# Four transformer layers on one core: the Mamba and expert stage with routers beside expert blocks, smaller exp blocks and a new order of pieces

## The chip, the cores and the metric

One Trainium2 chip, one of its cores. The metric is the device time of one execution in microseconds (us); lower is better.

## The reference, cut to what matters

`x` is 2 x 1024 tokens of 128 channels. Eight sub-layers follow each other, each as `x = x + layernorm(f(layernorm(x)))`. The change touches the first two:

```
# 1: Mamba, then a residual and a mixture of 8 experts, top 2
h  = rmsnorm(x);  xm, z = split(h @ W_in.T)          # 256 channels each
xc = silu(causal_conv4(xm) + conv_b)
dt, B, C = split(xc @ W_xproj.T)                     # 64, 16, 16
delta = softplus(dt @ W_dt.T + b_dt)                 # 256 channels
h[n] = exp(delta * A[n]) * h[n] + delta * B[n] * xc  # 16 states n, scanned along the tokens
y  = sum over n of h[n] * C[n] + D_skip * xc
x1 = x + (y * silu(z)) @ W_out.T
out = x1 + sum over 8 experts of w[e] * (silu(g @ gate[e]) * (g @ up[e])) @ down[e],  g = rmsnorm(x1)
# 2: 64 small experts (hidden 32, top 8) and 2 shared ones (hidden 256)
out = sum over e of c[e] * (silu(g @ W1[e] + B1[e]) @ W2[e] + B2[e]) + shared(g)
```

The others are an RWKV layer with a ternary projection, attention in a window of 32 with position-routed linear maps, and attention in Lorentz space with an MLP of one shared and 8 routed experts.

## The kernel before, in words

The 2,048 tokens are four groups of 512, held in SBUF as `X`. Every engine walks through one and the same list of pieces, `ORDER` (lines 95 to 149), and issues its own part of each piece; nothing else sets the order. A piece is a lane, a step and a group: `aF1.0` is step F1 of lane a for group 0. Queues run in order, so a wait in one piece holds up all pieces behind it on that engine. Waits are on semaphores that count steps, with group numbers folded in (`at_least`).

Lane a (`mamba_and_experts`) is the subject. Its **Mamba steps** for group i: F1, F5, F6 normalise (statistics and scaling on VectorE, the power on GpSimd, transposes on TensorE; L608 to L630); F2 and F0 project in, L441 and L444; F7 convolves, L642 and L644, and applies Silu; F3 projects to dt, B and C; F8 projects to delta, L456, and takes the softplus on ScalarE (Abs, Exp, Ln, L357 to L367) and VectorE; F4 spreads the first B row over the partitions (L461) with a selector matrix `sel`; F9 makes `delta * xc`. Then there are 16 states k: `Nk` makes the C row in PSUM bank S0 (L468), which ScalarE copies to `cb` (L371), and VectorE multiplies delta x with the B row in bank S2 (L691); `Aq` makes eight of the 32 exps of `delta * A` on ScalarE (L377); `nk` has two scans on VectorE (L698) into one of the buffers `hs` and the next B row (L471); `ok` keeps the last column for the next group with a VectorE copy (L703, groups 0 and 2, since a batch is two groups), multiplies `hs` with `cb` on GpSimd (L313) and adds the product to `cv` (L290). B1, B3, B4 and B2 gate, project out, add the residual and normalise. The normalised `XA` is kept for the experts.

Its **expert steps** for group e: R1, R3, R4 route to 8 experts (logits in bank E0, softmax and top 2 on VectorE, transposes in E0, three bf16 parts of the weights in `w3`); M0 to M15 are the blocks of the 8 experts, two for each: spread weight in bank E3 (L504), gate L507, up L510, Silu L399, product L752, down L557, and the weighing L854; L1 and L3 to L5 sum up and normalise; R2, R5, R6 route to 64 experts; U0 to U15 are four small experts each (L537, L543 and L544, Silu L414, product L809, down L563), U16 to U19 the shared ones; L2, L6, L7 end the layer. The Mamba of group g stands beside the experts of group g-1 in the list; the experts of group 3 stand beside the first RWKV pieces (lane b, steps K), the rest of which stand among the window attention (steps A, Q, C, N, V, H, W, O, X). Lane c is the last layer.

ScalarE holds one set of function tables at a time, and an ACT_TABLE_LOAD is issued where the next function is of another set (Exp, Ln, Silu). The selectors `sel` (96 x 4096) and `selE` (128 x 2048) are built by GpSimd in F5 of group 0, by four memsets and five selects (L259 to L270); semaphore `selectors` counts them. Two lines which the prediction follows:

```
L377  act.activation(dA[...], dl[...], ACT.Exp, scale=Aneg[...])       # for t in range(8 * k, 8 * k + 8)
L703  inc(V.tensor_tensor(carry[:, k, :], hs[:, k % HS, :, G - 1], hs[:, k % HS, :, G - 1], ALU.max))
```

Of the kernel before, what the change touches and what calls it, by code (L numbers as in the profile page):

```python
# [89 lines left out]
MAMBA_END = 130016  # L90
# [2057 lines left out]
```

## Time and profile before

| | us |
|---|---|
| median of 3 runs (1591.90 to 1593.06) | 1592.79 |
| the profiled execution | 1592.28 |
| its span in the trace | 1590.5 |
| TensorE busy | 1170.1 (74%) |
| VectorE busy | 1098.0 (69%) |
| ScalarE busy | 636.9 (40%) |
| GpSimd busy | 540.1 (34%) |

The profile is one execution. The trace lists each instruction with its engine (PE is TensorE, PEld its weight loads, DVE VectorE, ACT ScalarE, POOL GpSimd), the line of the kernel, the tiles, the start and the duration; an idle engine's row names what ended the idle time. PEclk is the granted TensorE clock as a share of full speed. The groups' Mamba fronts (F1) begin near 5, 150, 327 and 503 us; lane a's Mamba ends near 668 us, group 3's experts near 835 us.

### The profile page before, as it was taken

Reading aid. Unit: us, or ns where it says so; the run is one execution under the profiler, and the core shown is the slowest. Engines: PE = TensorE matmul, PEld = TensorE weight load, DVE = VectorE, ACT = ScalarE, POOL = GpSimd, SP = SyncE. Lnnn points to the kernel's source line nnn. Section 1 sums busy time; section 2 is a strip of 40 time slices with the busy share of each in tenths; the row PEclk is TensorE's granted clock in tenths of the full one; section 3 lists DMA queues with packets and bytes.
Section 4 is the critical chain, followed back from the end, with each engine's and each line's share of the span. In section 5 each row is a group of like instructions: output and inputs, shape, how many; then the busy total and the mean of one; then the engine's idle time right before and its main releaser. Section 6 shows DMA issues by size and latency. Waiting matters only on the chain.

```text
span 1590.5 us, 12969 instructions
## 1 busy us (share of the span) xinstructions
PE 1170.1 (74%) x3808; PEld 564.8 (36%) x3818; DVE 1098.0 (69%) x2497; ACT 636.9 (40%) x1147; POOL 540.1 (34%) x348
## 2 busy tenths in 40 slices
PE   2223784967477774969597686787978699999897
PEld 1001232323223331334233352435435255555553
DVE  6896787669897788666827898997787644444221
ACT  2530763337332663332321421413325056654443
POOL 6495185515753185601202222131321012112111
PEclk8555896978789896969797898998999899999999
DMA  5000000000000000020001000000000100000000
GB/s 190 0 0 0 0 1 0 1 0 1 0 1 0 1 1 0 7 85 0 1 0 60 1 1 1 1 1 1 0 1 1 60 0 1 7 1 7 1 7 7
DMA packets 11270, 17.75 MB, mean 11 GB/s; under 512 B 1304, under 2 KB 7584, under 8 KB 10688
## 3 DMA queue, kind: packets, MB, share of 16 engines
q1 hardware_dynamic: 11200, 16.93, 3.1%
q8 instruction: 30, 0.49, 0.1%
q14 instruction: 40, 0.33, 0.1%
HBM read 15.88 MB, written 1.05 MB: 11 GB/s over the span
## 4 chain that ended last, share of the span: by engine, by line
PE 30%; DVE 17%; ACT 3%; issue 2%; POOL 1%; POOLq 0%; DVEq 0%; ACTq 0%
PE bankE L1682 7%; PE bankE L1760 5%; DVE b_yt L1477 2%; PE bankE L1148 2%; PE bankS L1709 2%; PE bankS L1724 1%; DVE b_m L1436 1%; PE bankE L537 1%; DVE b_pT L1449 1%; PE bankE L1169 1%; PE bankS L1662 1%; DVE b_vh L1285 1%; PE bankE L563 1%; DVE c_tw L1852 1%; DVE b_xnS L1256 1%
## 5 line engine op out<-in xcount | busy, mean ns | idle before, releaser
L313 POOL TENSOR_TENSOR hc<-hs,cb 128x1024 f32<-128x1024 f32 x60 | 141.1, 2352 | 77.9 <-DVE hs L698 75.2
L698 DVE TENSOR_TENSOR_SCAN hs<-dA,carry,bankS 128x512 f32<-128x512 f32 x128 | 156.5, 1263 | 3.0 <-ACT dA L377 0.9
L1682 PE MATMUL bankE<-c_h,c_w 128*128 128x512 f32 x288 | 151.3, 608 | 7.7 <-DVE c_tw L1852 6.1
L1655 ACT ACTIVATE c_h<-bankE,C 128x512 f32<-128x512 f32 x144 | 99.0, 688 | 118.2 <-PE bankE L1760 117.9
L290 POOL TENSOR_TENSOR cv<-cv,hc 128x1024 f32<-128x1024 f32 x60 | 141.5, 2358 | 4.7
L1852 DVE SCALAR_TENSOR_TENSOR c_tw<-bankE,C,wb_ready 128x512 f32<-128x512 f32 x32 | 24.0, 750 | 123.3 <-PE bankE L1682 123.3
L1551 POOL TENSOR_TENSOR c_acc<-c_acc,c_tw 128x512 f32<-128x512 f32 x32 | 40.7, 1273 | 185.3 <-DVE c_tw L1852 185.3
L414 ACT ACTIVATE sg<-bankE,C 128x512 f32<-128x512 f32 x80 | 55.0, 687 | 120.8 <-PE bankE L537 120.8
L1760 PE MATMUL bankE<-c_fH,c_w1H 128*128 128x512 f32 x144 | 101.1, 702 | 0.0
L537 PE MATMUL bankE<-fT,f 128*128 128x512 f32 x128 | 76.1, 678 | 13.6 <-DVE c L802 13.6
L471 PE MATMUL bankS<-bc,sel 96*128 96x512 bf16 x60 | 28.9, 481 | 72.1 <-DVE hs L698 72.1
L377 ACT ACTIVATE dA<-dl,Aneg 128x512 f32<-128x512 f32 x128 | 80.1, 708 | 0.1
L691 DVE TENSOR_TENSOR bankS<-dx,bankS 128x1024 f32<-128x1024 f32 x64 | 78.1, 1220 | 1.0 <-PE bankS L471 0.8
L507 PE MATMUL bankE<-h2T,wg 128*128 128x512 f32 x128 | 72.3, 648 | 7.5 <-ACT sg L399 7.5
L1062 ACT ACTIVATE b_pr<-bankE,b_nm 128x160 f32<-128x160 f32 x128 | 48.4, 404 | 72.5 <-DVE b_nm L1438 72.5
L371 ACT ACTIVATE cb<-bankS 128x512 f32<-128x512 f32 x64 | 37.9, 592 | 93.4 <-PE bankS L468 93.4
L563 PE MATMUL bankE<-hh,f 128*128 128x512 f32 x128 | 69.6, 626 | 5.1 <-DVE hh L809 5.1
L557 PE MATMUL bankE<-hh,wd 128*128 128x512 f32 x128 | 67.7, 611 | 2.5 <-DVE tw L854 2.0
L1682 PEld LDWEIGHTS bankE<-c_h,c_w 128*128 128x128 f32 x288 | 51.4, 190 | 33.4 <-issue 15.4
L313 POOL TENSOR_TENSOR cv<-hs,cb 128x1024 f32<-128x1024 f32 x4 | 9.4, 2357 | 147.8 <-DVE hs L698 147.8
L1760 PE MATMUL bankE<-c_fL,c_w1H 128*128 128x512 f32 x144 | 57.7, 401 | 0.0
L1760 PE MATMUL bankE<-c_fH,c_w1L 128*128 128x512 f32 x144 | 57.5, 399 | 0.0
(483 smaller groups left out, 2738.9 us busy)
## 6 DMA issues: line engine op xcount, KB each, us to landing
c_w<-in_w SPq DMA_DIRECT2D x1, 2304.0 KB, 8.9
X<-in_x SPq DMA_DIRECT2D x4, 256.0 KB, 3.7
wg<-in_gate_T SPq DMA_DIRECT2D x1, 1024.0 KB, 7.7
wu<-in_up_T SPq DMA_DIRECT2D x1, 1024.0 KB, 9.9
f<-in_w SPq DMA_DIRECT2D x1, 1024.0 KB, 7.2
out<-X SPq DMA_DIRECT2D x4, 256.0 KB, 2.3
b_wq<-in_Wqkv SPq DMA_DIRECT2D x1, 768.0 KB, 4.4
g<-in_sw SPq DMA_DIRECT2D x2, 256.0 KB, 3.4
```

Of the source, the lines that this page charges most:

```text
L290: pool.tensor_tensor(cv[:, :, :], cv[:, :, :], hc[:, :, :], ALU.add).then_inc(s["y_acc"], 1)
L313: pool.tensor_tensor(dst[:, :, :], hs[:, k % HS, :, :], cb[:, k % 2, :].unsqueeze(1).to_broadcast([P, HV, G]), ALU.mult).then_inc(s["hc_re ...
L377: act.activation(dA[:, t % DA, :], dl[:, h, :], ACT.Exp, scale=Aneg[:, h * NS + n:h * NS + n + 1]).then_inc(s["dA_ready"], 1)
L507: pe.matmul(E[0][:, :], wg[:, k * P:(k + 1) * P], h2T[:, :], start=True, stop=True).then_inc(s["g_ready"], 1)
L537: pe.matmul(E[k % 2][:, :], w, fT[:, :], start=True, stop=True).then_inc(s["up_ready"], 1)
L557: mm = pe.matmul(E[2][:, :], wd[:, b, :], hh[:, b % 2, :], start=(b % FB0 == 0), stop=(b % FB0 == FB0 - 1))
L563: pe.matmul(E[2][:, :], f2[:, b, :], hh[:, b % 2, :], start=(b == 0), stop=False).then_inc(s["fdown"], 1)
L691: V.tensor_tensor(dbx[:, :, :], dx[:, :, :], S[2][:, :].unsqueeze(1).to_broadcast([P, HV, G]), ALU.mult).then_inc(s["dbx_done"], 1)
L698: V.tensor_tensor_scan(hs[:, k % HS, h, :], dA[:, (HV * k + q) % DA, :], dbx[:, h, :], carry[:, k, h:h + 1], ALU.mult, ALU.add).then_inc(s ...
L1655: act.activation(h[:, n % 3, :], E[k % 2][:, :], ACT.Gelu_apprx_tanh, bias=col("b1_3", k)).then_inc(s["c_h"], 1)
L1682: pe.matmul(E[2][:, :], w2[:, k, :], h[:, n % 3, :], start=(f == 0), stop=(f == FB3 - 1)).then_inc(s["c_down"], 1)
L1760: mm = pe.matmul(E[k % 2][:, :], wp[:, k * P:(k + 1) * P], fp[:, i % 2, :], start=(q == 0), stop=(q == 2))
```

## The change

- **Selectors.** GpSimd adds parts of the identity into `cb`, and ScalarE spreads them into `sel` and `selE` with two copies before its first piece.
- **Group 0.** For states 3, 7, 11 and 15 VectorE multiplies `hs` by the C row in PSUM into a new buffer `hv`; ScalarE's copy to `cb` and GpSimd's product fall away there.
- **Carry.** The copy of the last column is a ScalarE copy.
- **First normalisation.** Statistics, powers and result have their own buffers (`stF`, `mvF`, `powF`, `rsF`, `tF`, `xnF`); VectorE's part of F6 is in F5; `XA` holds two groups, so F5 of group i waits for step L4 of group i-2. `oT` is `hT`.
- **F8, F4, F9.** The delta projection writes banks S0 and S2 and doesn't wait for the split of B and C; the first B row is made in F9, after delta.
- **Routers.** They use bank E3, not E0; the gates of the M blocks and the spread weights share E0 and E3 in a ring; a weight is spread one expert later, so M0 and M1 need no router result. The shared experts are U0 to U3. `sg` has three buffers. The weighing moves behind the odd block.
- **Exps.** Four instead of eight in a piece: A0 to A7.
- **ORDER** is laid out anew (999 pieces for 983), in all lanes. In groups 1 to 3, R3 and R4 stand further back (in groups 2 and 3 between F8 and F4), two M blocks stand between F4 and F9. `F1` of a group stands right behind `B2` of the group before, as it did. RWKV pieces K4.1 to K17.1 stand among U5.3 to U17.3.

The start of the list before and after, and the code:

```diff
-    aF1.0 aF5.0 aF6.0 aF2.0 aF0.0 aF7.0 aF3.0 aF8.0 aF4.0 aF9.0 aN0.0 aA0.0 an0.0 ao0.0 aN1.0 an1.0 ao1.0 aN2.0 an2.0 ao2.0 aN3.0 aA1.0
-    aB3.0 aB4.0 aB2.0 aF1.1 aR1.0 aF5.1 aR3.0 aF6.1 aF2.1 aF0.1 aR4.0 aF7.1 aM0.0 aF3.1 aM1.0 aM2.0 aF8.1 aF4.1 aF9.1 aM3.0 aN0.1 aM4.0
-    aA0.1 an0.1 ao0.1 aN1.1 an1.1 aM5.0 ao1.1 aN2.1 aM6.0 an2.1 aM7.0 ao2.1 aN3.1 aM8.0 aA1.1 an3.1 ao3.1 aN4.1 an4.1 aM9.0 ao4.1 aN5.1
...
+    aF1.0 aF5.0 aF6.0 aF2.0 aF0.0 aF7.0 aF3.0 aF8.0 aF4.0 aF9.0 aA0.0 aN0.0 an0.0 ao0.0 aN1.0 an1.0 ao1.0 aA1.0 aN2.0 an2.0 aA2.0 ao2.0
+    an15.0 ao15.0 aB1.0 aB3.0 aB4.0 aB2.0 aF1.1 aR1.0 aF5.1 aM0.0 aF6.1 aF2.1 aF0.1 aR3.0 aF7.1 aR4.0 aM1.0 aF3.1 aF8.1 aF4.1 aM2.0 aM3.0
+    aF9.1 aA0.1 aN0.1 an0.1 aM4.0 ao0.1 aM5.0 aN1.1 an1.1 aM6.0 aM7.0 ao1.1 aA1.1 aN2.1 an2.1 aM8.0 ao2.1 aN3.1 aM9.0 an3.1 aA2.1 aM10.0
...
+    def by_vector(i, k):
+        return i == 0 and k % 4 == 3
...
-            for q in range(3):
-                pool.wait_ge(s["selectors"], n)
-                pool.affine_select(out=sel[:, :, :], in_=sel[:, :, :], compare_op=ALU.not_equal, fill=1.0, base=-32 * q,
-                                   pattern=[[-1, 32], [0, P]], channel_multiplier=1).then_inc(s["selectors"], 1)
...
+        for ins in (pool.tensor_tensor(cb[:, 0, 0:32], ident[:, 0:32], ident[:, 32:64], ALU.add),
+                    pool.tensor_tensor(cb[:, 0, 64:128], ident[:, 0:64], ident[:, 64:128], ALU.add),
+                    pool.memset(w3[:, :], 0.0), pool.memset(p16[:, :, :], -1.0)):
+            ins.then_inc(s["selectors"], 1)
...
+        act.wait_ge(s["selectors"], 5)
+        act.activation(sel[:, :, :], cb[0:96, 0, 0:32].unsqueeze(2).to_broadcast([96, 32, P]), ACT.Copy).then_inc(s["selectors"], 1)
...
+            elif p[0] == "o" and not ends_batch(i):
+                at_least(act, s["scan_done"], i, HV * NS, HV * (k + 1))
+                act.activation(carry[:, k, :], hs[:, k % HS, :, G - 1], ACT.Copy).then_inc(s["carry_kept"], 1)
             elif p[0] == "A":
-                for t in range(8 * k, 8 * k + 8):
+                for t in range(EXPS * k, EXPS * k + EXPS):
...
             elif p == "F8":
                 at_least(pe, s["dt_ready"], i, 1, 1)
-                at_least(pe, s["bc_split"], i, 1, 1)
-                for h in range(HV):
-                    pe.matmul(S[h][:, :], wdt[:, h * P:(h + 1) * P], dtT[:, :], start=True, stop=True).then_inc(s["dpre_ready"], 1)
-            elif p == "F4":
-                if i == 0:
-                    pe.wait_ge(s["selectors"], 9)
+                for h in range(HV):
+                    pe.matmul(S[2 * h][:, :], wdt[:, h * P:(h + 1) * P], dtT[:, :], start=True, stop=True).then_inc(s["dpre_ready"], 1)
+            elif p == "F9":
+                if i == 0:
+                    pe.wait_ge(s["selectors"], 7)
                 at_least(pe, s["bc_split"], i, 1, 1)
+                at_least(pe, s["delta_ready"], i, HV, HV)
                 pe.matmul(S[2][:, :], sel[:, 0, :], bc3[:, :], start=True, stop=True).then_inc(s["Bb_ready"], 1)
...
-            elif p[0] == "o":
+            elif p[0] == "o" and by_vector(i, k):
                 at_least(V, s["scan_done"], i, HV * NS, HV * (k + 1))
-                if not ends_batch(i):
-                    inc(V.tensor_tensor(carry[:, k, :], hs[:, k % HS, :, G - 1], hs[:, k % HS, :, G - 1], ALU.max))
+                at_least(V, s["Cb_ready"], i, NS, k + 1)
+                at_least(V, s["y_acc"], i, NS - 1, k - 4)
+                V.tensor_tensor(hv[:, :, :], hs[:, k % HS, :, :], S[0][:, :].unsqueeze(1).to_broadcast([P, HV, G]), ALU.mult).then_inc(s["hv_ready"], 1)
```

## Rows read from the trace of the kernel before

**Rows 1.** Busy time by stretch: start:end, length; then PE, PEld, DVE, ACT, POOL, clock.

```profile
57.00:137.00 80.00, 15.52 (x30) 1.97 (x30) 73.12 (x64) 27.08 (x46) 72.66 (x31) 0.50 0.00 0
150.00:191.00 41.00, 29.24 (x66) 12.80 (x65) 28.08 (x70) 21.55 (x31) 2.04 (x2) 0.77 0.00 1
191.00:327.00 136.00, 99.22 (x251) 38.56 (x253) 105.22 (x177) 59.62 (x92) 85.71 (x42) 0.86 0.00 0
368.00:503.00 135.00, 97.78 (x238) 37.98 (x241) 120.50 (x172) 58.20 (x90) 84.64 (x41) 0.85 0.00 0
503.00:549.00 46.00, 31.52 (x78) 13.87 (x77) 32.42 (x90) 24.45 (x35) 3.02 (x3) 0.81 0.00 1
549.00:668.00 119.00, 86.63 (x217) 33.79 (x220) 96.50 (x138) 54.70 (x85) 83.61 (x40) 0.84 0.00 0
668.00:835.00 167.00, 131.99 (x337) 57.42 (x339) 99.24 (x292) 52.18 (x79) 23.48 (x25) 0.83 0.06 22
835.00:1120.00 285.00, 212.22 (x981) 115.84 (x982) 241.35 (x664) 82.05 (x268) 67.10 (x61) 0.89 0.03 9
1290.00:1590.50 300.50, 278.46 (x936) 157.57 (x934) 100.85 (x296) 159.33 (x232) 53.68 (x45) 0.99 0.01 4
```

**Rows 2.** The timeline, group 0's start and group 1's convolution: start, duration, instruction.

```profile
4.21 0.23 ACT L329 ACTIVATE Aneg<-C 128x32 f32<-128x32 f32 x1 [2.19 <-DMA C<-in_cst]
...
7.31 1.11 DVE L623 TENSOR_SCALAR XA<-X,mvS,rsS 128x128 f32<-128x128 f32 x4
...
8.55 5.92 DVE L628 TENSOR_SCALAR xnS<-XA,rsS 128x128 f32<-128x128 f32 x4
...
14.71 11.78 POOL L265 TENSOR_SCALAR_AFFINE_SELECT sel<-sel 96x4096 bf16<-96x4096 bf16 x3
...
19.37 7.40 DVE L642 TENSOR_SCALAR cv<-xm,C 128x512 f32<-128x512 f32 x2 [4.90 <-ACT xm L345]
...
26.63 5.18 POOL L270 TENSOR_SCALAR_AFFINE_SELECT selE<-selE 128x2048 bf16<-128x2048 bf16 x2
26.69 8.30 DVE L644 SCALAR_TENSOR_TENSOR cv<-xm,C,cv 128x512 f32<-128x512 f32 x6
...
162.62 0.49 DVE L642 TENSOR_SCALAR cv<-xm,C 128x512 f32<-128x512 f32 x1 [1.54 <-ACT xm L345]
...
164.72 4.06 DVE L644 SCALAR_TENSOR_TENSOR cv<-xm,C,cv 128x512 f32<-128x512 f32 x6
```

**Rows 3.** Instruction groups: busy, mean ns; then L703's, ns least/median/most.

```profile
L698 DVE TENSOR_TENSOR_SCAN hs<-dA,carry,bankS 128x512 f32<-128x512 f32 x128 | 156.5, 1263 | 3.0 <-ACT dA L377 0.9
...
L691 DVE TENSOR_TENSOR bankS<-dx,bankS 128x1024 f32<-128x1024 f32 x64 | 78.1, 1220 | 1.0 <-PE bankS L471 0.8
...
L371 ACT ACTIVATE cb<-bankS 128x512 f32<-128x512 f32 x64 | 37.9, 592 | 93.4 <-PE bankS L468 93.4
...
L703 DVE TENSOR_TENSOR carry<-hs x32: 155/1216/2315, 59.1 to 487.0; 128x2 f32<-128x2 f32 x32
```

**Rows 4.** The timeline of group 1's front.

```profile
170.99 0.59 ACT L357 ACTIVATE dtT<-bankS 64x512 f32<-64x512 f32 x1 [0.47 <-PE bankS L450]
...
176.25 1.98 PE L456 MATMUL bankS<-dtT,wdt 64*128 64x512 f32 x4
...
189.44 1.28 ACT L377 ACT_TABLE_LOAD   x1
190.73 5.01 ACT L377 ACTIVATE dA<-dl,Aneg 128x512 f32<-128x512 f32 x8
```

**Rows 5.** Waits, 150 to 327 us: in total, times, longest.

```profile
DVE hh L752 <- ACT sg L399: 5.4, 8, 1.6
...
PE bankE L495 <- DVE wt L834: 4.1, 1, 4.1
PE bankE L529 <- DVE wt L791: 4.0, 1, 4.0
```

**Rows 6.** A wait of 690 to 835 us, and VectorE's busy time in 852 to 905.

```profile
DVE hh L809 <- PE bankE L544: 15.9, 8, 3.2
...
852.00:905.00 53.00, 38.98 (x120) 0.76 0.12 45
```

More of the change, by code:

```diff
@@ L195, in mamba_and_experts, with rows_by @@
     cb = sb("cb", [P, 2, G])
+    hv = sb("hv", [P, HV, G])
+    def by_vector(i, k):
+        return i == 0 and k % 4 == 3
+    def rows_by(vector, i, k):
+        return sum(by_vector(i_, k_) == vector for i_ in range(i + 1) for k_ in range(NS if i_ < i else k))
     carry = sb("carry", [P, NS, HV])
-    oT = sb("oT", [P, G])
-    XA = sb2("XA", [P, NG * T * P])
+    oT = hT
+    XA = sb2("XA", [P, 2 * T * P])
     stE, mvE = sb2("stE", [P, T, 6]), sb2("mvE", [P, T, 2])
@@ L228, in mamba_and_experts @@
     N_M, N_U = E0N * FB0, EB1 + SB1
+    RING, BEFORE, held = {}, {}, {}
+    for n, tenant in enumerate([("gate", 0), ("gate", 1)] + [t_ for x_ in range(E0N) for t_ in (("weight", x_), ("gate", 2 * x_ + 2), ("gate", 2 * x_ + 3))][:-2]):
+        place = 0 if n < 2 or n % 2 else 3
+        RING[tenant], BEFORE[tenant] = E[place], held.get(place)
+        held[place] = tenant
     def sync(sp):
@@ L434, in piece @@
                 at_least(pe, s["xh_ready"], i, 1, 1)
-                turn(S[0], xnS).then_inc(s["xhT_ready"], 1)
+                turn(S[0], xnF).then_inc(s["xhT_ready"], 1)
             elif p == "F2":
@@ L522, in piece @@
                 at_least(pe, s["fT_ready"], e, 1, 1)
+                at_least(pe, s["wb_ready"], e, E0N, E0N)
                 for j in range(T):
-                    mm = pe.matmul(E[0][:, j * E1N:(j + 1) * E1N], fT[:, j * P:(j + 1) * P], r1[:, :], start=True, stop=True)
+                    mm = pe.matmul(E[3][:, j * E1N:(j + 1) * E1N], fT[:, j * P:(j + 1) * P], r1[:, :], start=True, stop=True)
                 mm.then_inc(s["lg_ready"], 1)
@@ L550, in piece, with ring_free, spread_weight @@
                 turn(E[0], yT).then_inc(s["moT_ready"], 1)
+        def ring_free(e, kind, n):
+            if BEFORE[kind, n] is not None:
+                was, m = BEFORE[kind, n]
+                at_least(pe, *((s["sg_ready"], e, N_M) if was == "gate" else (s["wb_ready"], e, E0N)), m + 1)
+        def spread_weight(e, x_):
+            if x_ == 0:
+                at_least(pe, s["w3_ready"], e, 2, 1)
+            ring_free(e, "weight", x_)
+            pe.matmul(RING["weight", x_][:, :], sel[:, x_, :], w3[:, :], start=True, stop=True).then_inc(s["wbc_ready"], 1)
         def down0(e, b):
@@ L668, in piece @@
                     at_least(V, s["sp_abs"], i, HV, h + 1)
-                    inc(V.tensor_scalar(dl[:, h, :], S[h][:, :], col("b_dt", h), 0.0, ALU.add, ALU.max))
+                    inc(V.tensor_scalar(dl[:, h, :], S[2 * h][:, :], col("b_dt", h), 0.0, ALU.add, ALU.max))
                 for h in range(HV):
@@ L758, in piece @@
                 at_least(V, s["moT_ready"], e, 2, 1)
-                inc2(V.tensor_tensor(xnE[:, :], XA[:, cols(e, 0, G)], E[0][:, :], ALU.add))
+                inc2(V.tensor_tensor(xnE[:, :], XA[:, cols(e % 2, 0, G)], E[0][:, :], ALU.add))
                 wait2()
```

309 lines of the change are left out of this document (158 added, 151 removed).

## The prediction

> **What bounds the kernel now.** I read the stretches first. Beside group 0's scans VectorE is busy 73.1 of 80 us and GpSimd 72.7, TensorE next to nothing. In the three cycles in which the Mamba of group g stands beside the experts of group g-1 (150 to 668 us) no engine is full: a front (F1 to F9) has 41 us with VectorE busy 28 and TensorE 29, the scans behind it 136 us with 105 and 99; group 2's scans hold 120 of VectorE in 135. Group 3's experts alone (668 to 835) lean on TensorE, 132 of 167, the window-attention stretch (835 to 1120) on VectorE, 241 of 285 or 85%, and the last 300 us are TensorE's, 278, so nothing in the change can shorten those but what comes earlier [rows 1]. Then the start: GpSimd builds the selectors until 31.8 us, and every VectorE row beside it is long [rows 2]. Then the repeated instructions by their groups [rows 3], the front of group 1 [rows 4], and the waits inside the first cycle [rows 5].
>
> **Part 1, selectors.** Three selects of 3.9 us each and more are replaced by small adds on GpSimd and two ScalarE copies. Beside GpSimd, xnS takes 5.92 us for four instructions, where XA, the same shape just before, takes 1.11: -4.8. The convolution runs from 19.37 to 34.99 us, where group 1's runs from 162.62 to 168.78: 15.6 less 6.2, -9.4 [rows 2]. The copies: 592 ns for 512 elements [rows 3] and 230 for 32 [rows 2] give 0.75 ns per element, so 3.3 us (4096) and 1.8 (2048). ScalarE is free near 4.9 us, so it is done near 10.0; hT would be wanted at 8.55 + 1.1 + 1.1 = 10.8. I take nothing; if the copies start late or run long, up to +5.1. First comes what the rows show: the long instructions are tensor_scalar and scalar_tensor_tensor while GpSimd works, and the same are short later. The Trainium skill (SBUF — State Buffer, section Who interferes with whom) says that such instructions in their two-port mode, or with two SBUF inputs, and GpSimd exclude each other for a whole instruction. By that rule the whole excess goes with the selects, as in my sum.
>
> **Part 2, F8.** The delta projection starts at 176.25 us although dtT stood at 171.6 [rows 4]; the B and C split and expert matmuls were between. In group 0 only the split was: -2.5, and -0.9 more for A0 placed before N0. The matmul that moves from F4 to F9 now waits for delta, which it did in effect before (its successor N0 did); behind it on TensorE stand N0 and the M blocks. Group 0's front: -4.8 -9.4 -2.5 -0.9 = **-17.6**.
>
> **Part 3, group 0's scans.** VectorE has per state one product 1.22, two scans 2.52 and a carry copy of 1.22 median; together 4.96, the pace of the stretch (80 / 16 = 5.0). GpSimd has 31 instructions, 72.66 us, so 2.34 each [rows 1, 3]. The change takes the copy to ScalarE (27 us busy of 80) and four products of GpSimd to VectorE, at the 1.22 us of the product with one PSUM operand. VectorE: 16 x 3.74 + 4 x 1.22 = 64.7; GpSimd: 27 x 2.34 = 63.2, plus 2.5 until the first scan ends. Each state hands over between the two, so I add about 5: 70.5, **-9.5** (bounds -6 if handovers cost double, -13 at 67). In those four states TensorE's next C row waits for VectorE's product, not for ScalarE's copy, and GpSimd's add behind it too; both are off the pace by a state and sit in the 5. The next scan of a buffer now waits for ScalarE's carry copy as well; it is short (32 elements took 0.23 us [rows 2]) and nothing but exps is queued behind it. With part 1 and 2: **-27** (-20 to -31).
>
> **Part 4, the paired cycles.** The first two expert blocks and the four shared blocks need no router result, so they cover what TensorE now spends waiting for the routers' weights, 4.1 + 4.0 us a cycle [rows 5]. F8 gives 2.5, the third sg buffer half of the 5.4 us that VectorE waits for Silu [rows 5], 2.7. Together 13.3: I take all in the first cycle, half in each of the next two, since group 2's scans are at 89% of VectorE and cannot take up more. The carry copies of group 2 (16 x 1.22 = 19.5 us) leave VectorE; a quarter of that, -5, since ScalarE's copy waits for the scans with Silus queued behind it. Against it F9, which waits behind M2 and M3: a Silu and a table load [rows 4], +2 in all. Sum -13 -7 -7 -5 +2 = **-30**.
> The exps: four blocks of eight (5.01 us and two loads of 1.28, so 7.57) become eight of four (2.5 + 2.56 = 5.07): ScalarE has 10.3 us more per cycle. By the order list 36 table changes up to B2 of group 3 become 50, and with the rest of the experts 15 more; 15 x 1.28 = 19 us of ScalarE. It is busy 81 of 177 in a cycle [rows 1], so it has room, and shorter blocks hold the Silus up less each time. The Trainium skill (ScalarE: Activation LUTs, sections What ACT_TABLE_LOAD costs and Rules for kernel authors) tells one to group by table set, and puts a switch at 2.66 us with its drain; it speaks against this part, and by it ScalarE would have 40 us more.
> Bounds of the cycles: 0, if each freed wait only uncovers the next; -56, if VectorE fills them to the 85% of the attention stretch: its busy time is 133 (150 to 327) + 149 (a front's 28 and group 2's 120.5) + 129 (503 to 668), less 19.5 for the carries, 391 / 0.847 = 462 against 518 [rows 1].
>
> **Part 5, the rest of the order.** Group 3's experts gain the two router waits (-8), but K-lane pieces (K4.1 to K17.1) come in among the U blocks: TensorE +4; **-3** (-8 to +2). Those pieces leave the attention stretch; in the part that holds them VectorE has 39 us of work in 53 [rows 6], about a third theirs, 13: **-10** (-4 to -16). Some of layer 3 starts earlier: **-4** (0 to -8), as the end is TensorE's. The new buffers, XA of two groups (F5 waits for L4 of group i-2, which is long done) and F6's VectorE part inside F5: nothing, VectorE does the same work in the same place. No DMA is added or moved, so SP's queue is as it was; on GpSimd the pow instructions keep their places among the pieces, now free of the selects ahead of them.
>
> Sum: -27 -30 -3 -10 -4 = -74, from the profiled execution's 1592.3 us (span 1590.5), 0.5 under the median 1592.8: **1518 us**.
>
> **The rivals.**
> 1. **The cycles don't shorten.** VectorE in F9 waits for the Silus of M2 and M3 which now stand ahead, or hh waits for TensorE, as in group 3's experts, 15.9 us over eight [rows 6]; the routers' cover is used up by that. For it: no engine is full, so the chain passes between engines. Against: the waits in rows 5 are TensorE's. Sum without part 4: -44, 1548.
> 2. **The cycles shrink to VectorE.** Part 4 at -56: -100, 1492. For it: the whole order is laid out anew, not only the named waits. Against: GpSimd, busy 86 of 136 us in the scans with instructions of 2.34 us, must hand over as well.
> 3. **Slower: ScalarE becomes the chain.** In the three cycles 24 breaks of 5.07 us stand where 12 of 7.57 did, 122 against 91, +31, and each F9 waits a Silu, a load and a hand back, about 4.5, +13. If TensorE and VectorE stand through every break and the rest gains nothing, -27 + 44: 1609. It decides from 27 us of ScalarE on the path. Against: ScalarE has 96 us free per cycle.
> 4. **It doesn't do what it says.** The first normalisation is to stand among the scans, but in the new list F1 of g+1 still comes right behind B2 of g, so no gain of it is in my sum. Were it among them, each of its tensor_scalars would stand beside GpSimd's products, and four cost 5.92 and not 1.11 us [rows 2]. That changes no number here.
>
> **How the numbers follow.** Forecast 0.50 (1500 to 1540, from the terms' bounds), rival 1 0.25, rival 2 0.20, rival 3 0.04, and 0.01 for all gains given back, within 0.2%, which is about what a measurement can tell from no change. Range: from rival 2, 1492 less 10 for its other terms' bounds, to rival 1, 1548 plus 14: 1482 to 1562. Faster 0.95, same 0.01, slower 0.04.
>
> **What would show it.** The first VectorE scan near 39 us, not 57; xnS near 1.1 us for four and the convolution near 6; group 0's last scan near 110; carry copies on ScalarE; the cycles, F1 to F1, at about 165, 165 and 159 us where they are 177, 176 and 165 (150, 327, 503, 668); no wait of TensorE for wt (L495 and L529 of before) over 1 us; ScalarE near 660 us busy; the last 300 us unchanged. Wrong: ScalarE's copies ending after 12 us; F9's matmul waiting over 5 us for delta; cycles as long as before (rival 1) or under 155 (rival 2); table loads between long idle times of TensorE (rival 3).

## The result and the profile after

The changed kernel takes 1546.31 us (median of 4 runs, 1544.80 to 1549.05); the kernel before took 1592.92 us beside it. The ratio is 0.9703 (95% interval 0.9677 to 0.9729), 46.6 us less. The span of the profiled execution fell from 1590.5 to 1543.6 us.

To see where the 46.9 us of span went I cut both traces at one VectorE instruction that occurs once in a group: the sum of XA and the projected Mamba output in B4, "XA<-XA,bankS". It starts at 144.7, 320.8, 498.3 and 668.3 us before, and at 113.3, 280.6, 451.4 and 624.7 after (first and last start stand in these two rows, before and after):

```profile
L717 DVE TENSOR_TENSOR XA<-XA,bankS x4: 686/686/687, 144.7 to 668.3; 128x512 f32<-128x512 f32 x4
L756 DVE TENSOR_TENSOR XA<-XA,bankS x4: 680/684/689, 113.3 to 624.7; 128x512 f32<-128x512 f32 x4
```

So group 0 gave 31.3 us, the cycles of groups 1 to 3 gave 8.9, 6.6 and -3.3 (176.1, 177.5 and 170.0 before; 167.2, 170.9 and 173.3 after), and everything behind gave 3.3 (922.2, 918.9). Of the 12.2 us of the cycles, 10.4 lie in the fronts, from the cut to the next group's first scan (46.8, 47.5 and 50.9 us before; 41.8, 45.0 and 48.0 after).

Busy time by stretch of the kernel after, columns as in [rows 1]:

```profile
35.00:113.00 78.00, 20.06 (x37) 3.83 (x38) 65.40 (x56) 27.48 (x59) 63.39 (x27) 0.51 0.00 0
118.50:155.00 36.50, 26.97 (x62) 11.28 (x61) 26.89 (x71) 21.26 (x30) 2.04 (x2) 0.78 0.00 1
155.00:286.00 131.00, 98.32 (x251) 38.25 (x252) 105.13 (x165) 66.77 (x99) 85.08 (x41) 0.90 0.00 1
325.50:457.00 131.50, 99.73 (x248) 39.52 (x249) 104.81 (x162) 69.28 (x116) 85.02 (x41) 0.88 0.00 0
499.00:625.00 126.00, 96.83 (x245) 37.96 (x247) 100.73 (x141) 67.18 (x99) 83.97 (x40) 0.91 0.00 0
625.00:791.00 166.00, 125.78 (x331) 55.72 (x333) 110.80 (x329) 53.09 (x81) 25.35 (x27) 0.86 0.06 22
791.00:1073.00 282.00, 218.41 (x987) 121.68 (x986) 232.47 (x637) 82.43 (x270) 66.39 (x63) 0.87 0.03 9
1243.00:1543.60 300.60, 277.91 (x936) 158.78 (x934) 104.47 (x311) 158.19 (x231) 54.30 (x46) 0.97 0.01 4
```

Against [rows 1]: in group 0's scans VectorE is busy 65.4 and GpSimd 63.4 us, where they were 73 each. Group 2's scans have lost 16 us of VectorE's work (104.8 for 120.5), but only 3.5 us of their length (131.5 for 135). The last 300 us are as they were.

The start, timeline of the kernel after, to compare with [rows 2]:

```profile
4.99 3.62 ACT L347 ACTIVATE sel<-cb 96x4096 bf16<-96x4096 f32 x1
...
8.51 1.89 ACT L348 ACTIVATE selE<-cb 128x2048 bf16<-128x2048 f32 x1
8.62 0.87 DVE L663 TENSOR_SCALAR xnF<-XA,rsF 128x128 f32<-128x128 f32 x4
...
14.31 0.49 DVE L677 TENSOR_SCALAR cv<-xm,C 128x512 f32<-128x512 f32 x1 [4.81 <-ACT xm L359]
...
16.42 4.06 DVE L679 SCALAR_TENSOR_TENSOR cv<-xm,C,cv 128x512 f32<-128x512 f32 x6
```

ScalarE's two copies end at 10.40 us, 0.36 us before it is needed. xnF takes 0.87 us for four and the convolution is over at 20.48, not 34.99. Waits of TensorE in the three cycles of the kernel after (118 to 625 us):

```profile
PE bankE L449 <- DVE xnE L631: 36.8, 3, 12.7
PE bankE L593 <- DVE tw L894: 25.7, 21, 2.0
...
PE bankE L516 <- DVE wt L874: 4.5, 2, 2.2
```

and of the kernel before (150 to 668 us), the routers' two:

```profile
PE bankE L529 <- DVE wt L791: 13.7, 3, 5.6
...
PE bankE L495 <- DVE wt L834: 11.0, 3, 4.1
```

The routers' 24.7 us have become 4.5; in their place TensorE stands 25.7 us, 21 times, before the down projection (L593) for the weighed tile `tw`. That looks like the place where the gain of the cycles went. The run e_weigh says that it isn't.

### The profile page after: what moved, and what is told of

Same layout as the page of the kernel before. It is cut to its first block, busy times and chain, and to the rows that moved or that the text cites. A ratio compares the mean times of both kernels' runs of the same rounds, so it can differ in the third digit from the quotient of the medians.

```text
span 1543.6 us, 13061 instructions
## 1 busy us (share of the span) xinstructions
PE 1172.5 (76%) x3806; PEld 570.5 (37%) x3818; DVE 1059.8 (69%) x2469; ACT 660.3 (43%) x1191; POOL 508.6 (33%) x340
## 4 chain that ended last, share of the span: by engine, by line
PE 31%; DVE 15%; ACT 3%; issue 2%; POOL 0%; POOLq 0%; DVEq 0%; ACTq 0%
PE bankE L1722 8%; PE bankE L1800 5%; PE bankE L1188 3%; DVE b_yt L1517 2%; PE bankS L1764 2%; DVE b_m L1476 1%; PE bankS L1749 1%; PE bankE L1209 1%; DVE b_pT L1489 1%; PE bankE L599 1%; PE bankS L1239 1%; ACT b_pr L1102 1%; DVE c_tw L1892 1%; DVE b_pT L1296 1%; DVE b_vh L1325 1%
## 5 line engine op out<-in xcount | busy, mean ns | idle before, releaser
L324 POOL TENSOR_TENSOR hc<-hs,cb 128x1024 f32<-128x1024 f32 x56 | 131.7, 2352 | 59.0 <-DVE hs L735 56.5
L301 POOL TENSOR_TENSOR cv<-cv,hc 128x1024 f32<-128x1024 f32 x56 | 133.1, 2377 | 4.4
L593 PE MATMUL bankE<-hh,wd 128*128 128x512 f32 x128 | 70.2, 631 | 33.6 <-DVE tw L894 33.6
L525 PE MATMUL bankE<-h2T,wg 128*128 128x512 f32 x128 | 75.4, 674 | 6.3 <-ACT wb L438 6.3
L559 PE MATMUL bankE<-fT,f 128*128 128x512 f32 x128 | 72.1, 645 | 0.0
L1010 POOL TENSOR_TENSOR b_rsS<-b_powS,half 128x4 f32<-128x4 f32 x16 | 16.2, 1014 | 148.2 <-DVE b_powS L1284 148.2
L1722 PEld LDWEIGHTS bankE<-c_h,c_w 128*128 128x128 f32 x288 | 51.8, 190 | 32.8 <-issue 13.1
L385 ACT ACTIVATE cb<-bankS 128x512 f32<-128x512 f32 x60 | 35.2, 587 | 40.3 <-PE bankS L489 39.6
```

Of the source, the lines that this page charges most:

```text
L301: pool.tensor_tensor(cv[:, :, :], cv[:, :, :], (hv if by_vector(i, k) else hc)[:, :, :], ALU.add).then_inc(s["y_acc"], 1)
L324: pool.tensor_tensor(dst[:, :, :], hs[:, k % HS, :, :], cb[:, k % 2, :].unsqueeze(1).to_broadcast([P, HV, G]), ALU.mult).then_inc(s["hc_re ...
L525: pe.matmul(RING["gate", k][:, :], wg[:, k * P:(k + 1) * P], h2T[:, :], start=True, stop=True).then_inc(s["g_ready"], 1)
L559: pe.matmul(E[k % 2][:, :], w, fT[:, :], start=True, stop=True).then_inc(s["up_ready"], 1)
L593: mm = pe.matmul(E[2][:, :], wd[:, b, :], hh[:, b % 2, :], start=(b % FB0 == 0), stop=(b % FB0 == FB0 - 1))
L1722: pe.matmul(E[2][:, :], w2[:, k, :], h[:, n % 3, :], start=(f == 0), stop=(f == FB3 - 1)).then_inc(s["c_down"], 1)
```

## The experiments

Each row is one kernel, an edit of the changed one. The cuts are those of above; "rest" is from group 3's cut to the end of the span, us.

| run | median us | ratio to before (95%) | first scan | group 0's cut | cycles 1, 2, 3 | rest |
|---|---|---|---|---|---|---|
| before | 1592.9 | 1 | 56.7 | 144.7 | 176.1, 177.5, 170.0 | 922.2 |
| after | 1546.3 | 0.9703 (0.9677, 0.9729) | 35.6 | 113.3 | 167.2, 170.9, 173.3 | 918.9 |
| e_selectors | 1570.5 | 0.9859 (0.9825, 0.9893) | 51.1 | 129.4 | 169.3, 170.9, 173.3 | 922.3 |
| e_no_hv | 1562.1 | 0.9772 (0.9754, 0.9789) | 36.9 | 124.2 | 167.2, 172.6, 173.2 | 922.8 |
| e_carry | 1580.3 | 0.9875 (0.9822, 0.9929) | 35.3 | 121.4 | 168.3, 183.4, 176.4 | 930.7 |
| e_weigh | 1550.3 | 0.9739 (0.9705, 0.9772) | 36.5 | 114.4 | 166.5, 170.6, 173.3 | 933.6 |
| e_exps8 | 1573.4 | 0.9874 (0.9854, 0.9894) | 35.2 | 114.3 | 175.0, 173.5, 177.5 | 926.5 |
| e_router_back | 1581.4 | 0.9898 (0.9867, 0.9929) | 36.8 | 114.4 | 173.5, 178.0, 185.5 | 927.2 |
| e_m_after | 1575.1 | 0.9835 (0.9793, 0.9876) | 39.0 | 116.6 | 170.3, 174.4, 179.9 | 933.0 |
| e_norm_among | 1583.3 | 0.9911 (0.9880, 0.9943) | 38.6 | 123.3 | 177.6, 179.7, 176.4 | 930.5 |
| e_norm_gap | 1556.9 | 0.9744 (0.9725, 0.9763) | 37.5 | 116.8 | 173.8, 173.7, 173.9 | 920.7 |
| e_code_only | 1641.2 | 1.0291 (1.0268, 1.0314) | 38.7 | 117.1 | 200.9, 191.3, 194.5 | 937.4 |
| e_code_weigh | 1588.2 | 0.9942 (0.9919, 0.9964) | 38.7 | 117.1 | 187.0, 177.4, 179.2 | 932.6 |
| e_old_tail | 1556.8 | 0.9741 (0.9715, 0.9766) | 36.7 | 114.5 | 167.4, 172.7, 171.7 | 925.5 |

The kernel before, run beside the experiments, took 1594.1, 1599.6 and 1598.8 us in their three sets, so a ratio says more than a median; the expectations count from 1546. How far a number of the table repeats can be read from it: e_old_tail has the list of after up to R2 of group 3, and its cycles are within 2 us of it. The rest, however, is 919 us in after and 921 to 934 in the nine runs that leave the list behind that cut alone or nearly so. TensorE's clock explains most of that. These are the busy times of the rest in after and in e_weigh, columns as in [rows 1]:

```profile
624.70:1543.60 918.90, 759.73 (x2814) 410.66 (x2816) 572.99 (x1647) 346.64 (x710) 177.83 (x167) 0.91 0.03 11
624.80:1558.50 933.70, 774.94 (x2814) 418.25 (x2816) 574.96 (x1647) 346.74 (x710) 178.02 (x167) 0.89 0.03 11
```

The same 2,814 matmuls took 15.2 us longer at a granted clock of 0.89 than at 0.91, and the rest is nearly 15 us longer; e_m_after, e_carry and e_norm_among, the other three of the nine over 930, have a busy TensorE of 772.0, 769.6 and 768.9 us. (In e_router_back it is 758.2, so its 8 us are not the clock.) Such differences go into the ratios and medians, so I judge by the cuts. It also tells why medians lie above the times expected where the cuts agree with the forecast (e_selectors 1570.5 for at most 1568, e_no_hv 1562.1 for 1555): the expectations count from after, whose trace has one of the earliest starts and the shortest rest.

The start has a scatter of the same kind: nine of these runs leave the pieces up to the first scan as in after, and have it at 35.2 to 39.0 us. The last section shows why. Of the cut of group 0 and of the first scan only larger differences count, or such whose steps the trace shows.

### Group 0: selectors, products, carry

**e_selectors** puts GpSimd's four memsets and five selects back:

```diff
+                if i == 0:
+                    selectors()
...
-        act.activation(sel[:, :, :], cb[0:96, 0, 0:32].unsqueeze(2).to_broadcast([96, 32, P]), ACT.Copy).then_inc(s["selectors"], 1)
```

> The changed kernel with GpSimd's four memsets and five selects back in F5 of group 0 in place of the small adds and ScalarE's two copies. Forecast by my sum: xnF near 5.9 us for four, the convolution near 15 us long, the first scan 14 to 20 us later than the 35.6 us of the change; group 0's remaining work moves with it, since nothing later has slack to take it up: 1546 + 17 = 1563 (range 1558 to 1568). Rival: the delay is half absorbed, because the first group's scans then run beside a GpSimd that is not behind, or later groups catch up: 1550 to 1556.

Timeline of VectorE in this run:

```profile
8.09 5.92 DVE L671 TENSOR_SCALAR xnF<-XA,rsF 128x128 f32<-128x128 f32 x4
18.92 7.39 DVE L685 TENSOR_SCALAR cv<-xm,C 128x512 f32<-128x512 f32 x2 [4.90 <-ACT xm L367]
26.23 8.30 DVE L687 SCALAR_TENSOR_TENSOR cv<-xm,C,cv 128x512 f32<-128x512 f32 x6
```

The long rows of [rows 2] are back within 0.01 us, and the first scan is at 51.1, 15.5 us later than after; group 0's cut moves by 16.1, the first cycle is 2.1 us longer and the other two are the same. The forecast of the sum holds, the rival (half absorbed) falls. 1.4 of the 15.5 us are not VectorE's: from the start of F3's matmuls to `dtT` it is 3.38 us here and 1.97 in after, by the clock that the last section shows.

**e_no_hv** (`by_vector` returns False) and **e_carry** (below):

```diff
-            elif p[0] == "o" and not ends_batch(i):
-                act.activation(carry[:, k, :], hs[:, k % HS, :, G - 1], ACT.Copy).then_inc(s["carry_kept"], 1)
...
+                if not ends_batch(i):
+                    V.tensor_tensor(carry[:, k, :], hs[:, k % HS, :, G - 1], hs[:, k % HS, :, G - 1], ALU.max).then_inc(s["carry_kept"], 1)
```

> The changed kernel with all sixteen products of group 0 by C on GpSimd again. My sum: GpSimd's 31 instructions of 2.34 us take 72.6 us and set the pace at 4.7 us a state, where it is 4.0 now; group 0's first XA sum comes 8 to 10 us later than 113.3, and the cycles stay: 1546 + 9 = 1555. Rival (the scans and not GpSimd set the pace, as hs has several buffers): under 3 us.

> The changed kernel with the carry copy back on VectorE (two SBUF operands), in groups 0 and 2. My sum: group 0's scans go from 63 to about 76 us (16 copies of up to 1.22 us less what its slack hides, +10 to +16), group 2's cycle +5; 1546 + 18 = 1564. Rival: with the copy spread between the scans GpSimd, not VectorE, sets the pace in group 2, so that only group 0 grows: 1556 to 1560.

GpSimd at group 0's end in e_no_hv, timeline:

```profile
107.49 2.34 POOL L324 TENSOR_TENSOR hc<-hs,cb 128x1024 f32<-128x1024 f32 x1 [0.17 <-POOL cv L301]
109.91 2.34 POOL L301 TENSOR_TENSOR cv<-cv,hc 128x1024 f32<-128x1024 f32 x1
```

The busy times of its group 0, columns as in [rows 1]:

```profile
37.00:124.00 87.00, 21.28 (x38) 4.38 (x38) 60.20 (x51) 28.70 (x61) 72.68 (x31) 0.51 0.00 0
```

GpSimd's instructions stand back to back, 4.92 us a state; its last add is at 114.8 us, 12 us behind the last scan. From first scan to cut it is 87.3 us, where after has 77.7: the four products are worth 9.6, within the 8 to 10 expected, and the rival falls. The carry copies, in e_carry on VectorE and in after on ScalarE (ns least/median/most):

```profile
L737 DVE TENSOR_TENSOR carry<-hs x32: 147/950/2302, 37.8 to 463.6; 128x2 f32<-128x2 f32 x32
L388 ACT ACTIVATE carry<-hs x32: 189/204/206, 38.1 to 440.0; 128x2 f32<-128x2 f32 x32
```

In e_carry the distance from first scan to cut is 86.1, 8.4 more than after. In group 2's cycle the copies cost 12.5 us, where I had expected 5; the rival, by which only group 0 grows, falls. The two don't add up: before, with neither, the distance was 88.0, 10.3 more than after. A reason that fits the busy times of [rows 1] is that without either edit VectorE (73 us busy) and GpSimd (73) are equally late.

### The cycles: the weighing, the exp blocks, the router

**e_weigh**:

```diff
-                if k % FB0 == 1 and k > FB0:
-                    weigh(e, k // FB0 - 1)
                 if k >= 2:
                     at_least(V, s["down"], e, N_M, k - 1)
                 V.tensor_tensor(hh[:, k % 2, :], sg[:, k % SG, :], EU[k % 2][:, :], ALU.mult).then_inc(s["hh_ready"], 1)
+                if k % FB0 == 0 and k > 0:
+                    weigh(e, k // FB0 - 1)
```

> The changed kernel, but VectorE weighs expert x behind the product of block 2x+2, as before, and not ahead of the product of block 2x+3. In the trace after, TensorE waits for the weighed tile 7 times in each cycle, 8.3, 8.8 and 8.5 us, and 8.0 beside group 3; before, these waits were under 3 us. Theory A (the order puts the weighing behind a wait for the odd block's up projection, right ahead of the down projection that needs it, so TensorE stands once per expert and gives back what the routers saved): these waits fall to about 2 us a stretch, the cycles to about 161, 165 and 162 us, and the time to about 1546 - 22 = 1524. Theory B (the cycles go by the chain of scans and hand-overs on VectorE and GpSimd, TensorE has slack): the waits fall as well, the cycles stay within 2 us, 1543 to 1547. Theory C (VectorE is held up by a weighing that comes too early, since it waits for ScalarE's copy of the weight): waits of VectorE for wb of a us each, 1550 or more.

Waits of TensorE in its cycles, 118 to 625 us:

```profile
PE bankE L593 <- DVE tw L894: 12.7, 14, 1.3
```

The edit takes back the weighing of the changed kernel, which stands in the odd block ahead of its product, not behind the block as the description of the change says. The wait fell by 13.0 us, and group 3's cut stands at 624.8 against 624.7. Theory A falls, and so does my reading of the waits: 13 us of TensorE's waiting for `tw` were not on the path of any cycle. They were not won either: over the three cycles TensorE is idle for 126.7 us (510.4 less 383.7 busy), where it was 130.9 in after, so most of the idle time only came to stand before other instructions. Theory B holds for the cycles. The median of 1550.3 is above its 1543 to 1547; the profiled execution, at 1560.3, is the longest of the four, with the rest at the lower clock.

**e_exps8**: the same list, eight exps in every even piece, none in the odd. It also moves four of each eight exps forward to the piece before.

```diff
-                for t in range(EXPS * k, EXPS * k + EXPS):
+                for t in range(EXPS * k, EXPS * k + 2 * EXPS) if k % 2 == 0 else ():
```

> The changed kernel, but every even exp piece makes eight exps and every odd one none, so that the order is the same and the table changes fall by up to a half in the cycles. Theory A (the shorter blocks were worth having: Silu and copies wait 5.1 us and not 7.6 behind them): the cycles grow by 2 to 4 us each, 1550 to 1558. Theory B (the extra table loads take away as much as they give, the stated rule of grouping by table set holds): cycles shorter by 2 to 5 us each, 1532 to 1542, ScalarE's busy time down by about 15 us. Theory C (ScalarE has room either way): within 2 us, 1544 to 1548.

Table loads ahead of exps, first in e_exps8, then in the kernel after:

```profile
L394 ACT ACT_TABLE_LOAD  x13: 1283/1283/1283, 30.8 to 564.2; - x13
```

```profile
L394 ACT ACT_TABLE_LOAD  x19: 1283/1283/1283, 31.2 to 548.7; - x19
```

VectorE's wait for the Silus of the M blocks in the three cycles, in the same order:

```profile
DVE hh L793 <- ACT sg L412: 32.1, 15, 4.5
```

```profile
DVE hh L793 <- ACT sg L412: 15.3, 15, 4.2
```

ScalarE has 247.3 us of work in its three cycles and 263.0 in those of the kernel after, so fewer table changes do save it 16 us; and the cycles are 14.5 us longer. The wait of VectorE that grew most is the one for a Silu, by 16.8 us. Theory A has the sign right; the cycles grew by 7.8, 2.6 and 4.1 us, where it had 2 to 4. The edit doesn't part the length of the blocks from the place of the exps, and TensorE is busy 8.0 us longer on the same 933 matmuls (388.6 for 380.5), so how much of the 14.5 is the block length alone is open. The Trainium skill (ScalarE: Activation LUTs, section Rules for kernel authors) tells one to group by table set; the trace agrees that this saves ScalarE's time, and the cycles show that it didn't save the kernel's. The Trainium skill (ScalarE: Activation LUTs, section What ACT_TABLE_LOAD costs) puts a switch at 2.66 us, a load of 1.28 with a drain behind it. The drain is not seen in the trace after: at 26.04 us a load of 1.28 begins, and the next Exp starts at 27.34.

**e_router_back** moves R1, R3 and R4 of each group ahead of M0, which is also ahead of the next group's F6.

> The changed kernel with R1, R3 and R4 all ahead of M0 in each group. It measures the cover that M0 and M1 give the first router. Forecast of my sum: the 4.1 us wait of TensorE for wt comes back, and with it that of the parts of the weights, so +4 to +7 in each of three cycles, nothing beside group 3 (there the list has the router ahead of M0 anyway): 1558 to 1567. Rival (TensorE has slack in the cycles, as the weighing run showed: its waits fell by 13 us and no cycle moved): within 3 us, 1543 to 1549.

Waits of TensorE in it, 118 to 650 us:

```profile
PE bankE L517 <- DVE wt L875: 19.1, 3, 8.2
```

Cycles 6.3, 7.1 and 12.2 us longer, where I had expected 4 to 7; the rival (within 3 us in all) falls. Nearly all of it lies in the fronts, which take 46.7, 55.4 and 57.9 us for 41.8, 45.0 and 48.0. So the place of the router does count, unlike that of the weighing. The wait for `wt` grew by 14.6 us only (19.1 for 4.5), and the cycles by 25.7: the edit moves VectorE's and ScalarE's work of the router too, so the 25.7 us are the price of the whole move and not of that wait. What sets this wait apart, as the list has it, is what comes next behind it: the transposes and projections of the next group's front, which its scans need. That reason is argued, not shown by a run of its own.

**e_m_after** moves the M blocks between F4 and F9 behind N0.

> The changed kernel with the two M blocks that stand between F4 and F9 in groups 1 to 3 moved behind N0. My rival 1 blamed them: VectorE reaches delta times x of F9 only behind the products of both blocks, which wait for their Silus, and ScalarE's first exps come behind them. If so: from F8 to the first scan 4 to 6 us shorter, scans as long, 1546 - 12 = 1534. If they only fill the softplus chain, in which TensorE and VectorE would idle: the first scan is earlier, but the M blocks are later by as much, and the cycles grow by 0 to 5 us: 1546 to 1560.

VectorE in group 1's front:

```profile
150.76 1.23 DVE L728 TENSOR_TENSOR bankS<-dx,bankS 128x1024 f32<-128x1024 f32 x1
...
155.02 0.69 DVE L794 TENSOR_TENSOR hh<-sg,bankE 128x512 f32<-128x512 f32 x1 [3.03 <-ACT sg L413]
...
157.93 0.69 DVE L895 TENSOR_TENSOR tw<-bankE,wb 128x512 f32<-128x512 f32 x1 [2.22 <-PE bankS L529]
158.53 0.68 DVE L794 TENSOR_TENSOR hh<-sg,bankS 128x512 f32<-128x512 f32 x1
159.13 2.45 DVE L736 TENSOR_TENSOR_SCAN hs<-dA,carry,bankS 128x512 f32<-128x512 f32 x2
```

The product for the scan is made 11.7 us after `dtT` (139.1) and 18.1 in the kernel after (135.7, 153.8), so F9 did wait 6 us for the two blocks. But the scan then waits for them: from cut to first scan it is 42.5, 50.0 and 53.5 us, not shorter than the 41.8, 45.0 and 48.0 of the kernel after, and the cycles are 3.1, 3.5 and 6.6 us longer. The blocks were filling the softplus. Rival 1's wait was there, but taking it away gains nothing.

### The first normalisation among the scans

**e_norm_among** puts F1 of the next group behind n11 and F5 behind n14; **e_norm_gap** F1 behind n13 and F5 behind B1.

> The changed kernel with F1 of the next group moved behind n11 and F5 behind n14 of the group before, for groups 1 to 3, so that the first normalisation does stand among the scans, as the description of the change has it. In the trace after, the statistics of group 1 begin at 117.5 us and TensorE's turn of xnF comes at 124.9, though it could follow the turn of xnS at 118.8. Theory A (the front is a chain, and 6 us of it go): each cycle 4 to 6 us shorter, in total 1546 - 15 = 1531. Theory B (VectorE's eight tensor_scalars then stand beside GpSimd's products and wait for them, and VectorE also waits inside F5 for a power that is queued on GpSimd behind a product): single tensor_scalars of 1 to 2.5 us in place of 0.3, scans 6 to 10 us longer per cycle, 1546 to 1560.

> The changed kernel with F1 of the next group behind n13 and F5 behind B1 of the group before. There the statistics stand among the scans, but the tensor_scalars stand where VectorE waits for the output projection and GpSimd has no product left (in group 0, 109 to 113 us of the trace after). Theory A (what spoiled the run with F5 behind n14 was the contention and GpSimd's queue, not the idea): tensor_scalars at 0.3 us, TensorE's turn of xnF right behind that of xnS, fronts 4 to 6 us shorter, cycles (first XA sum to first XA sum) at about 163, 167 and 169 us for 167, 171 and 173: 1546 - 12 = 1534. Theory B (any VectorE work put on the way of group g delays its B4 by as much): fronts shorter, the end of the group later, 1542 to 1550.

VectorE's F5 in e_norm_among, in groups 0 and 1:

```profile
100.51 2.20 DVE L656 TENSOR_SCALAR powF<-tF 128x4 f32<-128x4 f32 x1
...
103.86 5.03 DVE L664 TENSOR_SCALAR xnF<-XA,rsF 128x128 f32<-128x128 f32 x4
...
275.91 1.11 DVE L659 TENSOR_SCALAR XA<-X,mvF,rsF 128x128 f32<-128x128 f32 x4
277.16 5.03 DVE L664 TENSOR_SCALAR xnF<-XA,rsF 128x128 f32<-128x128 f32 x4
```

xnF takes 5.03 us for four, where it takes 0.87 after; one instruction of 128x4 elements takes 2.20 for 0.17. That agrees with the exclusion that the Trainium skill tells of (SBUF — State Buffer, section Who interferes with whom), at a new place. Group 0 grows by 7 us from first scan to cut and the cycles by 10.4, 8.8 and 3.1: theory B. In e_norm_gap xnF is short again (0.87 for four), but nothing is gained: the cycles are 6.6, 2.8 and 0.6 us longer. Theory A falls, and theory B's shorter fronts are not there either (44.3, 44.7 and 47.3 us). TensorE's turns of xnS and xnF there, and in the kernel after:

```profile
121.07 1.11 PE L450 MATMUL bankS<-ident,xnS 128*128 128x128 f32 x4 [4.35 <-DVE xnS L766]
...
128.31 1.06 PE L450 MATMUL bankS<-ident,xnF 128*128 128x128 f32 x4
```

```profile
117.65 1.11 PE L449 MATMUL bankS<-ident,xnS 128*128 128x128 f32 x4 [4.37 <-DVE xnS L765]
...
124.88 0.76 PE L449 MATMUL bankS<-ident,xnF 128*128 128x128 f32 x4
```

They are 7.24 and 7.23 us apart: R1 and M0 stand between them in the queue, and they fill the time whether xnF is ready or not. That tells why there is no gain. Of the 10 us of loss 7 lie in the scans, among which F1 now stands; in group 0's one of its instructions of 128x4 elements takes 1.89 us for 0.17. An early normalisation would need F6 ahead of M0 as well; that wasn't tried.

### The list of pieces

**e_code_only** is the new code under the list of before (an old block of eight exps is two of four side by side), **e_code_weigh** the same with the weighing of e_weigh, **e_old_tail** has before's list from R2 of group 3 on.

> The code of the changed kernel with the list of pieces of before (each old block of eight exps is two of four side by side). It tells what the new order is worth by itself. Theory A (the gain is in the start, group 0 and in the routers' cover that the new order uses): F1 of group 1 near 120 us all the same, the cycles near 175, 176 and 165 as before, in total about 1546 + 14 = 1560. Theory B (the order is worth little or nothing, since its shorter exp blocks cost what its router places gain): 1543 to 1550. Theory C (the new code needs the new order, M0 and M1 behind the router waste its cover and the later weighing costs 8 us a cycle): over 1570.

> The changed code with the list of before (that run took 1641 us, cycles of 202, 195 and 185 us) and the weighing back behind the even block. TensorE waited 44.0 us for the weighed tile there, VectorE 35.7 us for the up projection. Theory A (the new code loses under the old list by its later weighing): cycles fall by 10 to 20 us each, to 1590 to 1605. Theory B (it loses by another thing: pairs of M blocks are split by the scans in the old list, so that a ring of banks shared by gates and weights waits for a Silu far behind in ScalarE's queue): 1630 or more.

> The changed kernel with the list of before from R2 of group 3 on, so that K4.1 to K17.1 stand in the attention stretch again and not among the U blocks, and the shared blocks wait behind the router. The gain that I gave to this part (-10 in the attention stretch, -4 in layer 3, -3 beside group 3) would be lost: 1546 + 15 = 1561. Rival (in the trace after, the time from group 3's XA sum to the end is 918.9 us, before 922.3, so this part is worth some 3 us): 1545 to 1552, the time behind the XA sum within 5 us.

The first wait of TensorE and the first of VectorE in e_code_only, 118 to 625 us:

```profile
PE bankE L594 <- DVE tw L895: 44.0, 21, 5.1
...
DVE hh L794 <- PE bankE L529: 35.7, 15, 3.7
```

The new code under the old list is 47 us slower than the kernel before (theory C), and 43 of the 75 us that its cycles are longer than after's go with the weighing (theory A of e_code_weigh), which under the new list made less than 1 us of difference. So the new code needs the new list. The old code under the new list wasn't run. With the old weighing the new code's cycles are still 19.9 us longer than those of before (543.5 for 523.6); 18.4 of that lie in the fronts (51.8, 52.5 and 59.3 us). Which edit is at fault there is open. e_old_tail's rest is 6.6 us longer than after's, though TensorE is busy 9.1 us less in it (750.6): it is idle 16 us more. The clock favoured this run, so the new tail is worth something; 6.6 is more than the rival's 5 and less than the 15 that I had expected, and with clocks that differ it is no exact price.

## Why the prediction was right, and where it wasn't

The time, 1546.3, lies in the range, 28 us over the point and above the 1500 to 1540 that the forecast had for itself. It is nearest to rival 1's 1548, but not by rival 1's way. The direction and the gain at the start were foreseen; that the time fell inside the range is owed to the width that rival 1 gave it. In the terms of the sum: group 0 gave 31 for 27, the cycles 12 for 30, parts of group 3 and behind 3 for 17.

- **Part 1, selectors, -14.2 and copies at nothing.** Right. Undone it costs 15.5 at the first scan, 1.4 of it by TensorE's clock, so 14.1. The copies took 3.62 and 1.89 us for my 3.3 and 1.8.
- **Part 2, -3.4.** Both terms right: from the start of `dtT` to the first scan it is 17.7 us before and 12.95 after, -4.75. The projection starts 0.05 us behind `dtT` where it started 2.58 behind it, so 2.5 as in the sum. With A0 ahead of N0 the exps' table load is done within the softplus (it ends at 32.4 us, before delta at 33.1), and the scan starts 2.6 us behind delta where it took 3.4: 0.8 for my 0.9. The other 1.4 us are the clock, which the sum didn't have: the delta projection's four matmuls took 3.41 us before and 1.98 after.
- **Part 3, group 0's scans, -9.5.** Right: from first scan to cut 88.0 before, 77.7 after, -10.3. Both causes showed, GpSimd's four products (e_no_hv) and the long copy (e_carry).
- **Part 4, the cycles, -30.** The step that failed. Measured -8.9, -6.6 and +3.3, -12.2. The failing sentence is "Together 13.3: I take all in the first cycle, half in each of the next two": it adds waits of different engines as if each were on the path. The experiments show that such a sum isn't sound: moving the router costs more than its wait (e_router_back), and halving the wait for `tw` gains nothing (e_weigh). I also left the later weighing unpriced; under the new list that did no harm, under the old one it costs 43 us. That more and shorter exp blocks are no loss was right; e_exps8 puts them, with the place of the exps, at 14.5 us. Singly undone, the router's place, the carry copies and the exp blocks come to 57 us against a gain of 12, so these parts don't add up; which part of the new list or code gives the difference back is open.
- **The third cycle.** It got longer, most likely since the list gives it more to do (read from the traces, not tested): group 2's experts end 10.6 us behind the cut (step L7's sum at 635.3), before 26.9 (695.2). I had counted the blocks but given this no price. It brought group 3 nothing: from the cut to its last sum it is 183.7 us for 183.4, where I had -3. Its 16 M blocks now take 63 us (Silus 655.7 to 718.5) and took 50 (714.4 to 764.8), with K2, K3 and K13 among them.
- **Part 5, -10 and -4.** Oversized: what follows group 3's last sum takes 735.2 us for 738.9, -3.7. The clock plays no part here, as TensorE is busy 759.8 us behind the cut before and 759.7 after. VectorE's busy time in the attention stretch fell by 9 us (232.5 for 241.4), the stretch by 3.
- **Rival 3** (ScalarE) is refuted by e_exps8, **rival 2** by the cycles' 167 to 173 us. **Rival 4** was right in what it says of the list, and e_norm_among gives its price: 7 us in group 0 and 22 in the cycles.

## What to carry to other kernels

Don't take the price of a wait from its length, and don't add up waits of different engines: halving 26 us of TensorE's waits before a down projection moved no cycle, and the router put ahead of the projections that feed the scans cost 6 to 12 us a cycle. Where an engine with many kinds of work in its queue (here ScalarE) serves another that waits for it, shorter blocks can be worth more than the table loads that they cost. A hand-planned order and the code under it must be judged together; undoing single parts of such a pair costs more than the whole gained (e_carry, e_exps8 and e_router_back cost 57 us together in the cycles, the gain was 12). And before a difference of a few us is explained, compare TensorE's busy time for the same matmuls: it can be the clock.

## What the runs showed of the hardware that I had not expected

Part of the start's gain in these two traces is TensorE's clock. Busy time and clock (next to last but two) of 35 to 39 us before, and of 20 to 23 us after, in both of which the four matmuls of F3 run:

```profile
35.00:39.00 4.00, 3.70 (x4) 0.96 (x4) 0.20 (x2) 0.78 (x3) 0.00 (x0) 0.50 0.00 0
```

```profile
20.00:23.00 3.00, 1.93 (x4) 0.57 (x4) 0.96 (x3) 1.55 (x3) 0.00 (x0) 1.00 1.00 385
```

Before, TensorE had stood 12.25 us waiting for the convolution, and the granted clock was 0.50, the lower level of 1.2 GHz; the matmuls took 3.70 us. After, it had stood 3.27 us and ran at 1.00: 1.93 us. It would be easy to say that the shorter stall keeps the clock up. The other runs don't bear that out. Here are the same four matmuls in e_carry and in e_m_after, whose starts are those of after:

```profile
20.42 1.93 PE L468 MATMUL bankS<-xc,wx 128*96 128x512 f32 x4 [3.58 <-ACT xc L368]
```

```profile
20.45 3.70 PE L472 MATMUL bankS<-xc,wx 128*96 128x512 f32 x4 [3.17 <-ACT xc L369]
```

With as short a stall e_m_after had the lower level: its clock is 0.50 from 20 to 27 us. Over the nine runs with this start the four matmuls take from 1.93 to 3.70 us, and the first scan, at 35.2 to 39.0 us, is late where these matmuls or those of the delta projection are slow. So the kernel after was lucky by up to 3 us in its profiled start, and what decides the level there is open.
